# Four graph layers in one kernel: the product x W1 moved into the eigenvalue sweeps, and an unrolled spectral stage

## What is computed

```python
_, U = jnp.linalg.eigh(L_norm)
agg = jnp.einsum('mn,bnd->bmd', U.T, features)
h = jax.nn.relu(agg @ W1 + b1)           # 256 -> 128
out = h @ W2 + b2                        # 128 -> 256
x = _layernorm(x + jnp.einsum('nm,bmd->bnd', U, out))
# layer 1 begins with
h = jax.nn.relu(jnp.einsum('ts,bsh->bth', adj, x @ Wg0 + bg0))
h = jax.nn.relu(jnp.einsum('ts,bsh->bth', adj, h @ Wg1 + bg1))
```

## Time and profile before

| | |
|---|---|
| median of 3 runs | 2397.5 us (2396.79 to 2400.31) |
| the profiled execution | 2398.23 us |
| its span in the trace | 2396.4 us |
| busy in the span | PE 75%, PEld 61%, DVE 63%, ACT 36%, POOL 29% |
| DMA busy, 40 slices of 60 us, tenths | 6000000000000010000000000000004112200101 |
| sweeps | first at 226.6 us, last at 437.0 us |
| spectral stage | 549.9 to 866.3 us |

### The profile page before, as it was taken

How to read it: one execution, slowest core, us unless ns; L and a number is a source line. 1 busy time by engine, 2 the same in 40 slices (tenths; PEclk the granted TensorE clock), 3 DMA queues, 4 the chain that set the end, 5 groups by cost and what they waited for, 6 DMA issues and landing times. The chain is left out here.

```text
span 2396.4 us, 33303 instructions
## 1 busy us (share of the span) xinstructions
PE 1800.0 (75%) x9260; PEld 1470.4 (61%) x9260; DVE 1501.1 (63%) x5902; ACT 862.2 (36%) x1754; POOL 684.6 (29%) x1065
## 2 busy tenths in 40 slices
PE   3443000006999979999999999999997998878775
PEld 2332000004767658888889999888886886656553
DVE  7999999883554536644444444443444777757885
ACT  2332111001333336633333333332223666456563
POOL 0011444201111047633333332422230115323332
PEclk9999999999999999999999999999998999989998
DMA  6000000000000010000000000000004112200101
GB/s 171 1 2 1 1 1 1 1 0 18 26 31 30 27 36 18 13 9 9 9 14 10 9 0 9 0 0 0 18 0 158 62 62 83 71 9 26 35 34 36
DMA packets 44658, 62.24 MB, mean 26 GB/s; under 512 B 13969, under 2 KB 33297, under 8 KB 44433
## 3 DMA queue, kind: packets, MB, share of 16 engines
q1 hardware_dynamic: 43968, 61.05, 7.5%
q10 hardware_dynamic: 592, 0.17, 0.0%
HBM read 36.04 MB, written 25.17 MB: 26 GB/s over the span
## 5 line engine op out<-in xcount | busy, mean ns | idle before, releaser
L1889 ACT ACTIVATE l_gates<-ps,biases 128x512 f32<-128x512 f32 (+1 forms) x504 | 289.4, 636 | 501.9 <-remote 487.4
L1823 PE MATMUL ps<-l_nodes_in,l_even 128*128 128x512 f32 x1392 | 319.2, 389 | 0.5 <-remote 0.4
L1823 PE MATMUL ps<-l_nodes_in,kept 128*128 128x336 f32 (+1 forms) x1280 | 300.4, 352 | 9.0 <-remote 7.1
L1823 PEld LDWEIGHTS ps<-l_nodes_in,l_even 128*128 128x128 f32 x1392 | 261.0, 188 | 55.4 <-issue 1.3
L1934 DVE TENSOR_TENSOR l_gates<-l_gates 128x512 f32<-128x512 f32 (+1 forms) x72 | 49.9, 693 | 343.1 <-ACT l_gates L1889 343.1
L1778 POOL CAST l_nodes_in<-big 128x512 fp32r (+3 forms) x142 | 101.7, 745 | 546.4 <-remote 529.9
L1823 PEld LDWEIGHTS ps<-l_nodes_in,kept 128*128 128x128 f32 x1280 | 230.8, 189 | 35.7 <-issue 12.1
L1823 PE MATMUL ps<-l_state,l_even 128*128 128x512 f32 x960 | 220.8, 389 | 0.0
L1823 PEld LDWEIGHTS ps<-l_state,l_even 128*128 128x128 f32 x960 | 180.2, 188 | 37.4
L1781 POOL TENSOR_TENSOR l_nodes_in<-big,l_nodes_in 128x512 fp32r<-128x512 f32 (+1 forms) x142 | 200.9, 1435 | 5.7
L960 PE MATMUL ps<-sw_one,tab 64*1 64x1 f32 x4 | 0.4, 161 | 226.6 <-DVE sw_one L630 217.6
(11 more groups left out here) (525 smaller groups left out, 4005.8 us busy)
## 6 DMA issues: line engine op xcount, KB each, us to landing
x<-in_x SPq DMA_DIRECT2D x4, 2048.0 KB, 17.0
residual<-s_x SPq DMA_DIRECT2D x16, 512.0 KB, 2.7
x_late<-residual SPq DMA_DIRECT2D x16, 512.0 KB, 9.5
normed<-j_x SPq DMA_DIRECT2D x16, 512.0 KB, 2.6
x_late<-normed SPq DMA_DIRECT2D x16, 512.0 KB, 3.2
out<-a_y SPq DMA_DIRECT2D x16, 512.0 KB, 2.9
l_raw<-in_L_gnn_W SPq DMA_DIRECT2D x16, 256.0 KB, 2.7
l_raw<-in_L_gnn_W SPq DMA_DIRECT2D x4, 512.0 KB, 3.8
```

What stands on the lines that cost most here:

```text
L1823: return pe.matmul(ps[:, 4 * j + gate, 0:n], w[w_part][:, at:at + 128].bitcast(F32R), src[:, part, k, 0:n].bitcast(F32R), start=start, sto ...
L1889: act.activation(gates[:, j, gate, 0:n], ps[:, 4 * j + gate, 0:n], ACT.Tanh if gate == G else ACT.Sigmoid, bias=bias[:, gate * KD + j:gate ...
```

## The change

In the sweeps, TensorE turns each group of x (8 transposes against the identity) and multiplies it with W1. ScalarE moves the turned group to `sw_xT` after every even sweep and the product to `big[:, 0, :]`, 128 features for each token, after every odd one. The wait for the early transfers moves from SyncE to TensorE.

In the spectral stage layer 0 is computed as U^T (x W1): one matmul of 512 columns mixes the 128 features of a group (`spread`), VectorE adds b1, ScalarE applies the ReLU, the hidden layer is mixed back (`mix_hidden`, four 128x128 matmuls) and only then multiplied with W2 (`out0`). So `a0`, `hidden`, `back0`, and the copies of x are gone. b2 enters through the row sums of U: GpSimd adds the product of both to x in place (`shift_x`). The stage is written out step by step, without hardware loops, and its semaphores count up instead of being cleared. `CountedNorm`, so far used by a later stage, moves up in the file and gains `normalise_vector`.

```diff
+    xT = ctx.enter_context(nc.sbuf_tensor("sw_xT", [128, KD, GROUP], F32))
+    XT, XW = ps[:, 2:4, :], ps[:, 4, :]
+    xt_ready, xt_moved, xw_ready, xw_moved = (sem(s) for s in ("xt_ready", "xt_moved", "xw_ready", "xw_moved"))
...
+            def move_turned(g):
+                act.wait_ge(xt_ready, g + 1)
+                if g:
+                    act.wait_ge(xw_ready, g)
+                act.activation(xT[:, :, :], XT, ACT.Copy).then_inc(xt_moved, 1)
+
+            def move_product(g):
+                act.wait_ge(xw_ready, g + 1)
+                act.activation(big[:, 0, g * GROUP:(g + 1) * GROUP], XW, ACT.Copy).then_inc(xw_moved, 1)
+
             for i in range(FIRST_SWEEPS):
                 sweep(i + 1, i)
+                if i % 2 == 0:
+                    move_turned(i // 2)
+                else:
+                    move_product(i // 2)
...
+            landed(pe)
+            for g in range(GROUPS):
+                if g:
+                    pe.wait_ge(xt_moved, g)
+                for k in range(KD):
+                    for i in range(TILES):
+                        mm = pe.transpose(XT[:, k, i * TILE:(i + 1) * TILE],
+                                          x[:, g * TILES + i, k * 128:(k + 1) * 128], t["ident"][:, :])
+                mm.then_inc(xt_ready, 1)
+                pe.wait_ge(xt_moved, g + 1)
+                if g:
+                    pe.wait_ge(xw_moved, g)
+                for i in range(TILES):
+                    for k in range(KD):
+                        mm = pe.matmul(XW[:, i * HID0:(i + 1) * HID0], xT[:, k, i * TILE:(i + 1) * TILE], w1[:, k, :],
+                                       start=k == 0, stop=k == KD - 1)
+                mm.then_inc(xw_ready, 1)
...
+            dve.tensor_reduce(m["rowsum"][:, :], ps[:, 1, 0:N], AX_X, ALU.add).then_inc(u_moved, 1)
...
+    A1 = C = ps[:, 0:2, :]
+    B, Z = ps[:, 2:4, :], ps[:, 4:6, :]
+    G, Z = (pair.rearrange("p a (b n) -> p (a b) n", b=2) for pair in (B, Z))
+    SPREAD, MIXED = ps[:, 6, :], ps[:, 7, :]
+    STEPS = GROUPS + 3
...
+            def spread(g):
+                if g:
+                    pe.wait_ge(u_summed, g)
+                pe.matmul(SPREAD, m["spread"][:, :], big[:, 0, g * GROUP:(g + 1) * GROUP], start=True,
+                          stop=True).then_inc(u_ready, 1)
+            def mix_hidden(g):
+                pe.wait_ge(hid_ready, g + 1)
+                if g:
+                    pe.wait_ge(uh_moved, g)
                 for i in range(TILES):
-                    mm = pe.matmul(Y[:, i, :], hid[:, i * TILE:(i + 1) * TILE], w["w2"][:, :], start=True, stop=True)
-                mm.then_inc(y_ready, 1)
-
-            def back0(pair_in_use):
-                if pair_in_use:
-                    pe.wait_ge(c_free, 1)
-                    pe.sem_clear(c_free)
-                pe.wait_ge(y_moved, 1)
-                pe.sem_clear(y_moved)
-                for i in range(0, TILES, 2):
-                    mm = pe.matmul(Z[:, i:i + 2, :], m["spreadT"][:, :], y[:, i:i + 2, :], start=True, stop=True)
+                    cols = slice(i * TILE, (i + 1) * TILE)
+                    mm = pe.matmul(MIXED[:, cols], hid[:, cols], m["spreadT"][:, :], start=True, stop=True)
+                mm.then_inc(uh_ready, 1)
...
+            def out0(g):
+                pe.wait_ge(uh_moved, g + 1)
+                if g:
+                    pe.wait_ge(ln.added, g)
...
+            for s in range(STEPS):
+                if s < GROUPS:
+                    spread(s)
+                if 2 <= s < GROUPS + 2:
+                    aggregate2(s - 2)
+                if s < GROUPS:
+                    mix_hidden(s)
+                if 1 <= s < GROUPS + 1:
+                    aggregate1(s - 1)
+                if s < GROUPS:
+                    out0(s)
+                if 1 <= s < GROUPS + 1:
+                    convolve1(s - 1)
+                if 2 <= s < GROUPS + 2:
+                    convolve2(s - 2)
...
+            for s in range(STEPS):
+                if s < GROUPS:
+                    relu0(s)
+                if 2 <= s < GROUPS + 2:
+                    move_b(s - 2)
+                if s < GROUPS:
+                    move_mixed(s)
+                if 1 <= s < GROUPS + 1:
+                    move_a1(s - 1)
+                if s >= 3:
+                    relu2(s - 3)
+                if 1 <= s < GROUPS + 1:
+                    relu1(s - 1)
...
+            def bias0(g):
+                dve.wait_ge(u_ready, g + 1)
+                if g:
+                    dve.wait_ge(hid_ready, g)
+                dve.tensor_tensor(summed[:, :].rearrange("p (t f) -> p t f", t=TILES),
+                                  SPREAD.rearrange("p (t f) -> p t f", t=TILES),
+                                  w["b1"][:, None, :].to_broadcast([128, TILES, HID0]), ALU.add).then_inc(u_summed, 1)
...
+            def norm(g):
+                dve.wait_ge(z_ready, g + 1)
+                dve.wait_ge(x_shifted, g + 1)
+                ln.add(dve, g, Z, tiles_of(g))
+                ln.statistics(dve, g)
+
+            def normalise(g):
+                if g:
+                    dve.wait_ge(a1_ready, g)
+                    dve.wait_ge(x1_stored, 16 * g)
+                ln.normalise_vector(dve, g, x1)
...
+            for s in range(STEPS):
+                if s < GROUPS:
+                    bias0(s)
+                    norm(s)
+                if 1 <= s < GROUPS + 1:
+                    bias1(s - 1)
+                if s < GROUPS:
+                    normalise(s)
+                if 2 <= s < GROUPS + 2:
+                    bias2(s - 2)
...
+            def shift_x(g):
+                pool.tensor_tensor(tiles_of(g), tiles_of(g),
+                                   shift_out[:, None, :].to_broadcast([128, TILES, WIDTH]), ALU.add).then_inc(x_shifted, 1)
+
+            pool.tensor_scalar(shift_out[:, :], w["b2"][:, :], m["rowsum"][:, :], None, ALU.mult).then_inc(shift_ready, 1)
+            pool.wait_ge(shift_ready, 1)
+            shift_x(0)
             ln.begin(pool)
-            stage(0)
-            with pool.Fori(0, GROUPS - 1) as g:
-                pool.wait_ge(xin_free, 1)
-                pool.sem_clear(xin_free)
-                stage(g + 1)
-                ln.power(pool)
-            ln.power(pool)
+            for g in range(GROUPS):
+                if g + 1 < GROUPS:
+                    pool.wait_ge(u_summed, g + 1)
+                    shift_x(g + 1)
+                ln.power(pool, g)
...
+            for g in range(GROUPS):
+                sp.wait_ge(ln.written, TILES * (g + 1))
+                sp.dma_start(residual[g], x1[:, :, :]).then_inc(x1_stored, 16)
             sp.dma_start(raw, source).then_inc(raw_landed, 16)
+            sp.wait_ge(x1_stored, 16 * GROUPS)
```

More of the change, by code:

```diff
@@ L1462, in spectral_and_mixing, with tiles_of @@
-    Y, G, Z = (pair.rearrange("p a (b n) -> p (a b) n", b=2) for pair in (Y, G, Z))
+    def tiles_of(g):
+        return x[:, g * TILES:(g + 1) * TILES, :]
     with nc.Block() as block:
@@ new lines, in out0, with aggregate1 @@
+            def out0(g):
+                pe.wait_ge(uh_moved, g + 1)
+                if g:
+                    pe.wait_ge(ln.added, g)
+                for i in range(TILES):
+                    mm = pe.matmul(Z[:, i, :], mixed[:, i * TILE:(i + 1) * TILE], w["w2"][:, :], start=True, stop=True)
+                mm.then_inc(z_ready, 1)
+            def aggregate1(g):
+                if g >= 2:
+                    pe.wait_ge(c_summed, KD * (g - 1))
+                for i in range(TILES):
+                    pe.wait_ge(ln.written, TILES * g + i + 1)
+                    for k in range(KD):
+                        mm = pe.matmul(A1[:, k, i * TILE:(i + 1) * TILE], x1[:, i, k * 128:(k + 1) * 128],
+                                       m["mixT"][:, :], start=True, stop=True)
+                mm.then_inc(a1_ready, 1)
@@ L1569, in _ @@
         @block.scalar
         def _(act):
-            def move(src, dst, taken, given, func=ACT.Copy, **more):
-                act.wait_ge(taken, 1)
-                act.sem_clear(taken)
-                act.activation(dst, src, func, **more).then_inc(given, 1)
-            def first():
-                move(A0, agg0[:, :, :], a0_ready, a0_moved)
-            def relu0():
-                move(H, hid[:, :], hid_ready, hid_moved, ACT.Relu, bias=w["b1"])
-            def second():
-                move(A1, agg1[:, :, :], a1_ready, a1_moved)
@@ L1585, in relu1 @@
-            def relu1():
-                move(g1sum[:, :, :], h1[:, :, :], g_summed, h1_ready, ACT.Relu)
-            def third():
-                move(B, agg1[:, :, :], b_ready, b_moved)
-            def relu2(g):
-                act.wait_ge(c_summed, 1)
-                act.sem_clear(c_summed)
-                act.activation(group(big, g), h2sum[:, :, :], ACT.Relu).then_inc(c_used, 1)
-            def step(g, layer0, second_group, third_group, ahead):
-                if layer0:
```

(41 more changed lines are left out.)

311 lines of the change are left out of this document (111 added, 200 removed).

## The result

The changed kernel takes 2326.25 us (median of 4 runs, 2322.72 to 2328.98), the kernel before 2397.14 beside it: ratio 0.9701, with an interval of 0.9684 to 0.9718. The profiled execution took 2326.09 us.

What follows compares the result with a forecast made beforehand. TensorE's instruction count was taken to bound the old spectral stage. Head 15.9, two steps 30.2, 13 steps 189.2 and tail 24.3 gave 259.6 us against 316.4; less 0.2 for small edits, 56.6 us saved: 2341 us, range 2335 to 2347.

Steps and rivals of the forecast that it cites:

- a loop of waits: Spectral stage, mid-stage: a loop through four engines takes over from TensorE and sets the step at 14.55 us.
- the free work in the sweeps: Eigenvalue sweeps: the added TensorE work and ScalarE moves cost nothing; bounded from above at 27 us.
- rival 2: Spectral stage: only TensorE's work counts, step 14.2 us, neither start at half speed; kernel 2329 us; chance 0.10.
- Semaphore clears and loop ends vanish: Spectral stage: their removal was costed at nothing, since TensorE's bursts already touch.
- TensorE's 14.2 us: Spectral stage: TensorE's work in a new step, 17.66 us less 5.23 removed plus 1.75 added.
- 13 steps: Spectral stage, after the first two steps: 13 steps of 14.55 us, 189.2 us.
- The two steps: Spectral stage, after the head: two steps without second bias, 13.1 us each, plus 4 for a half-speed start: 30.2 us.
- The tail: Spectral stage, from the last normalisation to the end: 22.6 us, or 24.3 with a half-speed burst after a bare wait.
- The head: Spectral stage, from its start to the first normalisation: 12.4 us plus 3.5 for half-speed bursts, 15.9.
- rival 1: Spectral stage: a collision with GpSimd or slower hand-overs make the step 15.4 us; kernel 2354 us; chance 0.16.
- The sweeps didn't stretch: Eigenvalue sweeps: a rival had them stretch by their moves, 27 us more, kernel 2368 us; chance 0.04.
- The array lost no speed in mid-stage: Spectral stage: a rival had TensorE at half speed in every step, 28.4 us, kernel 2568 us; chance 0.02.

Runs made afterwards that it cites:

- shift_late: The changed kernel, but GpSimd does its power and shift before the addition to x, which then starts together with VectorE's normalisation: 2353.18 us, ratio 0.982.

## Why the prediction was wrong, and where it was right

**Right:** what bounds the kernel before, which bursts go and come (5.23 and 1.75 us, to 0.01), that a loop of waits comes within a few per cent of TensorE's work and where it closes, the first bias inside GpSimd's time, the normalisation at 1.38 us without a collision, the free work in the sweeps, and that everything later stays as it was. The step is a near tie that TensorE wins. That was rival 2 (14.2 us a step, 2329), priced at 0.10, though only in its first half: it also had neither start at half speed, and parts of both were.

**The step that failed:** "Semaphore clears and loop ends vanish, which I cost at nothing, since TensorE's bursts already touch". That reason holds for the step before, which TensorE sets (loop ends: 0.08 us). It doesn't hold for the loop that takes over, whose terms were read from rows with clears in them: 5.24 for 4.86, 0.40 for 0.20. These two are 0.58 of the 0.96 us by which the loop of 14.55 is longer than the measured 13.59; the rest is small terms of the table above, some with clears in them, some not. Without these two the forecast loop would be 13.97 us, below the 14.2 of TensorE's work and not above it.

**Second,** TensorE's 14.2 us was mis-sized by 0.25: the 0.55 us in brackets was taken as the pause's whole price, and it was 0.80. With both terms mended the step is the longer of 13.93 and 13.59, and 13 steps are 8.0 us shorter than forecast. The loop alone mended would have given 14.2 us a step and 4.6 of these 8.0; TensorE's work alone, none.

**The two steps** miss by 4.0: their loop is 12.31 us (578.52 to 590.83 between normalisations) and not 13.1, which makes 1.6, and the half-speed start cost 1.6 (the step before takes 13.88, 564.64 to 578.52) and not 4. At 567.34 and 569.21 two bursts take 1.87 and 2.51 us instead of 0.89 and 1.78, and the third is at full speed again; I had the rest of the group's bursts slow as well. **The tail** misses by 2.0: 1.7 of it is a half-speed burst that didn't come. No burst of the new tail follows a pause as long as the 2.69 us of before; the last convolution starts after 1.11 us and takes 3.70 us, full speed. **The head** was right in kind, all three of its first products at half speed (3.78 us for 8 instructions of 256 columns against 1.89), and forecast 1.1 us too long, of which 0.46 lies between add and normalisation (4.78 us, 559.86 to 564.64) and the rest in the hand-overs.

The rivals: there was no collision. When one was made the time was 2353, near rival 1's 2354, but that is luck: rival 1 added 13 us to a base of 2341, and the collision added 27 to 2326. The sweeps didn't stretch. The array lost no speed in mid-stage (granted 1.00). It did in the sweeps, where the granted clock averages 0.64, between the levels of 1.2 and 2.4 GHz, and that cost nothing. The Trainium skill (TensorE: Matmul & The Clock Gate, Part 1) has the half rate as the default state, from which activity releases the array. The sweeps agree with it, and so do both stage starts: from 549 to 560 us the granted clock is 0.50 and the products take twice their time. The column of the granted clock isn't enough by itself: in the kernel before it reads 1.00 from 551 to 555 us, where the burst of the earlier trace rows took 3.42 us instead of 1.95.

**The range** stopped at 2331, short even of rival 2's 2329, and no case had TensorE's own 14.2 us lower. The prediction says itself that other bursts show a shorter hand-over than 0.40, and kept the longer one for every hand-over from TensorE without carrying the shorter into the range. The row that it names for 0.40 gives 0.50.

**Where the 71.9 us of the stage come from,** by a mid-stage step: 3.48 of the 4.27 us are the work removed, and 0.80 the old pause and what it cost around it; that the new loop stays under TensorE's work is what lets both count. The clears matter little for the gain by themselves: putting those of the normalisation back costs 0.20 us a step, and the loop with all 13 is 14.49 us long.

## What to carry to other kernels

When work is taken from the engine that sets the step, sum the loop that comes next from rows in the form that it will have: here semaphore clears cost nothing beside a busy TensorE and 0.05 to 0.09 us each, in the mean, on a loop of waits. Price a pause by the distance of starts around it against the same burst without one, not by the idle time in brackets. Where two limits come as close as 14.55 and 14.2 us, let the range reach to the lower one with its own terms at their lower bounds.

## What was not expected of the hardware

A semaphore clear on the loop costs 0.05 to 0.09 us in the mean (13.59, 14.15 and 14.49 us for none, 6 and 13). A TensorE pause that the row gives as 0.55 us costs 0.80, 0.16 of it hidden in how the row's end is counted. A GpSimd addition of 2.35 us lengthens four tensor_scalar instructions from 1.38 to 3.29 us, a copy of 1.04 us to 2.22. The Trainium skill (SBUF — State Buffer, Who interferes with whom) has the shared port pair as an exclusive lock: whoever issues first holds it for the whole instruction, and the other is blocked. Both rows agree with it, the added time (1.91 and 0.84 us) being a little less than GpSimd's instruction, and so does the first normalising instruction of each: it ends 0.16 us after the addition in `shift_late` (690.79 and 690.63) and 0.15 us after the copy in the kernel before (1.25 us from 678.30, to 679.55, and 679.40). Its row there begins 0.06 us ahead of the copy's and it waits all the same, so the rows don't show which of the two issued first.
